# The attention's output product in three fp16 products instead of one fp32 product, with its scales, parts and squares placed among other work

## The chip, the cores and the metric

One core of one Trainium2 chip runs the whole program. The time is the device time of one execution in microseconds (us); less is better. TensorE (PE) multiplies, VectorE (DVE), ScalarE (ACT) and GpSimd (POOL) do elementwise work, SyncE (SP) starts most transfers.

## What is computed

Two graph layers on `x` (1250 rows of 512 features) with 20000 edges. The change is in the first one. Cut to what matters:

```python
h = relu(layernorm(x))                                   # layer 0 works on h
agg = segment_sum(batchnorm(h)[src], dst) / max(deg, 1)
conv_out = relu(agg @ W_conv + b_conv)
q, k, v = heads(h_dense @ Wq), heads(h_dense @ Wk), heads(h_dense @ Wv)   # h_dense: 256 rows
kv = einsum(phi(k), v);  z = 1 / (phi(q) @ sum(phi(k)) + KEPS)
attn = (einsum(phi(q), kv) * z) @ Wo                      # 256x512 @ 512x512
x = x + batchnorm(conv_out + attn[batch, pos] + h)
# layer 1: x + relu(bn(relu(bn(((1+eps) h + sum of h[src]) @ W1 + b1)) @ W2 + b2)), h = relu(layernorm(x))
```

## The kernel before, in words

TensorE counts the edges into a 1250x1250 matrix `AT`: 25 windows of 50 columns (line 1816), ten small fp16 matmuls each. Between windows stand pieces of the attention and the convolution. The order is the hand-written table `SLOTS` (line 79): one string a window. `G0` to `G9` are the ten tiles of the convolution, `K`, `Q`, `V` the projections, `UK`, `UQ`, `MX`, `QT`, `KV`, `O` the pieces of each pair of heads, `A00` to `A33` the aggregation by feature block and columns, `TA0` and `TA1` the transposes of `attn`, `WO0` and `WO1` the product with Wo. Each engine walks the table in this order in its own program, every queue strictly in order, and they meet at semaphores: `full` and `free` of the eight PSUM banks, and `s_...` of single steps.

- ACT (line 801) does in a slot: the pieces' copies out of PSUM, then the copy of `AT`, then extra work by a slot number (`conv_weights_high`, `weight_squares`, `weight_high`), and last the exponentials of `UQ` and `MX`, which are called late. `QT0` on PE (slot 8) transposes what the exponentials of `UQ0` wrote (slot 6) and waits for both heads of it (`s_eq`, line 1752). `G0` stands behind it in slot 9 and waits for POOL's `hn` (line 576).
- DVE (line 1290) makes the one-hot rows of the windows, reductions, the low parts and the sums into `hT`. After the windows it does `weight_low(0, 1)` (line 1140), `aggregate_terms()` (1148 to 1152) and the pieces of the last slot `TA0 TA1 A21 WO0 WO1` and of `LAST`, `A31 F2 DX2 A02 A12 A22 A23 A32 A33`.
- Most products are already split: `split3` (PE) sums hi·hi, hi·lo and lo·hi of fp16 parts. The product with Wo is not: `wA` and `attnT` are fp32, and each fp32 matmul is two instructions in the trace.

```python
for j in range(2):
    f = 2 * int(name[2]) + j
    for k in range(FB):
        ins = mm(ps[:, j * MAXN:(j + 1) * MAXN], wA[:, k, f * P:(f + 1) * P], attnT[:, k, :],
                 k == 0, k == FB - 1)
```

`F1` is the small product that sums the squares of W1 over the partitions for its scale; its square is taken by `weight_squares` on ACT and its inverse root by POOL (586, 587).

Of the kernel before, what the change touches and what calls it, by code (L numbers as in the profile page):

```python
# [63 lines left out]
for _n, _k in PARAMS:  # L64
# [14 lines left out]
SLOTS = [s.split() for s in (  # L79
# [4 lines left out]
SQ_AT, SPLIT_AT, H_AT, EDGES_OF_AT = 4, 7, 7, 18  # L84

SPARE = {"start": 18, "hT0": 3, "hT1": 4}
# [22 lines left out]
def unit_cols(name):  # L109
# [12 lines left out]

PAIR_BANKS = {f"UK{g}": (2, 3) for g in range(4)} | {f"{u}{g}": (4, 5) for g in range(4) for u in ("UQ", "QT")}
LONE_BANKS = {name: bank for bank, names in enumerate((
# [3 lines left out]
    for name in names.split()}  # L128
# [52 lines left out]

SQ1_AT, HIGH1_AT = (20, 21), (23, 24)
RAW = [name for slot in SLOTS for name in slot if name[0] == "A"]
OUT_TILES = [(0, 4), (4, 8), (8, 10)]

# [33 lines left out]
def gnn_kernel(nc, x, src, dst, params, eps, w_conv, wq, wk, wv, wo, proj, w1, w2, out):  # L221
    with ExitStack() as ctx:
# [95 lines left out]
        wB = place("wB", [P, FB, D], F32, 162)  # L318
        vaug = place("vaug", [P, 2, HEADS, DH + 1], F32, 170)
        attn = place("attn", [P, 2, D], F32, 174.25)  # L320
        attnT = place("attnT", [P, FB, MAXN], F32, 178.25)
        HR = T
        hring = place("hring", [L, HR, D], F32, 182.25)
        x_in = [place(f"x_in{n}", [L, 2, D], F32, at) for n, at in enumerate((45, 49, 53, 57, 61))]
# [179 lines left out]
        def _(pool):  # L504
# [75 lines left out]
            pool.wait_ge(sem("s_bn0"), 2)  # L580
            for i in range(T):
                normed(i)
            for layer in range(2):
                pool.wait_ge(sem(f"s_mean_w{layer}"), 1)
                m, s = mean_w[layer], scale_w[layer]
                own.step(pool.tensor_scalar(m[:, 1:2], m[:, 0:1], 1e-30, None, ALU.add))  # L586
                pool.tensor_tensor(s[:, 0:1], m[:, 1:2], minus_half[:, 0:1], ALU.pow).then_inc(sem(f"s_scale_w{layer}"), 1)
# [54 lines left out]
        def _(act):  # L642
# [25 lines left out]
            def attention(name):  # L668
# [14 lines left out]
                elif name in ("Q0", "Q1", "K0", "K1"):  # L683
                    a, f = "QK".index(name[0]), 2 * int(name[1])
                    ps = read_group(act, name)[:].rearrange("p (f n) -> p f n", f=2)
                    copy(tqk[:, a, f:f + 2, :], ps, SCALE).then_inc(sem("s_tqk"), 1)
                    free_group(act.activation(sq[:, a, f:f + 2, :], ps, ACT.Square, scale=SCALE), name)
                elif name[:2] == "MX":
                    g = int(name[2])
                    act.wait_ge(sem("s_nbk"), g + 1)  # L690
                    if g == 0:
                        act.wait_ge(full[PLACE["hT9"][0]], PLACE["hT9"][1] + 1)
                    if g >= 2:
                        act.wait_ge(full[PLACE[f"KV{g - 2}"][0]], PLACE[f"KV{g - 2}"][1] + 1)
                    for j, h in enumerate(heads_of(name)):
                        ps = read_group(act, f"UK{g}.{j}")
                        act.activation(kf[:, h % 4, 0, :], ps[:, 0:M], ACT.Exp, bias=nbk[:, h, 0:1])
                        act.activation(kf[:, h % 4, 1, :], ps[:, M:], ACT.Exp, bias=nbk[:, h, 1:2])\
                           .then_inc(sem("s_ek"), 1)
                    for j, h in enumerate(heads_of(name)):  # L700
                        act.wait_ge(sem("s_ek"), h + 1)
                        act.sem_inc(free[PLACE[f"UK{g}.{j}"][0]], 1)
                        act.activation(kf[:, h % 4], kf[:, h % 4], ACT.Identity, bias=keps[:, 0:1], scale=1.0 / 16)\
                           .then_inc(sem("s_kf"), 1)
                elif name[:2] == "UQ":
                    g = int(name[2])
                    if g:
                        act.wait_ge(full[PLACE[f"QT{g - 1}.1"][0]], PLACE[f"QT{g - 1}.1"][1] + 1)
                    else:
                        act.wait_ge(full[PLACE["hT5"][0]], PLACE["hT5"][1] + 1)  # L710
                    for j, h in enumerate(heads_of(name)):
                        act.wait_ge(sem("s_nbq"), h + 1)
                        ps = read_group(act, f"UQ{g}.{j}")
                        act.activation(qf[:, h % 2, 0, :], ps[:, 0:M], ACT.Exp, bias=nbq[:, h, 0:1])
                        act.activation(qf[:, h % 2, 1, :], ps[:, M:], ACT.Exp, bias=nbq[:, h, 1:2])\
                           .then_inc(sem("s_eq"), 1)
                        act.wait_ge(sem("s_eq"), h + 1)
                        act.sem_inc(free[PLACE[f"UQ{g}.{j}"][0]], 1)
                elif name[:2] == "KV":
                    g = int(name[2])  # L720
                    ps = read_group(act, name)
                    free_group(copy(kv[:, 2 * g:2 * g + 2], ps[:, 0:4 * (DH + 1)]
                                    .rearrange("p (h m d) -> p h m d", h=2, m=2)), name)
                elif name[:2] == "QT":
                    g = int(name[2])
                    if g:
                        act.wait_ge(full[PLACE[f"O{g - 1}"][0]], PLACE[f"O{g - 1}"][1] + 1)
                    for j in range(2):
                        ps = read_group(act, f"{name}.{j}")
                        free_group(act.activation(qfT[:, j], ps[:].rearrange("p (m n) -> p m n", m=2), ACT.Identity,  # L730
                                                  bias=keps[:, 0:1], scale=1.0 / 16), f"{name}.{j}")
                elif name[:2] == "TA":
                    nt = int(name[2])
                    ps = read_group(act, name)
                    free_group(copy(attnT[:, :, nt * P:(nt + 1) * P],
                                    ps[:].rearrange("p (f n) -> p f n", f=FB)), name)

            def conv_weights():
                act.wait_ge(sem("d_wC"), 16)
# [2 lines left out]
            def conv_weights_high():  # L742
                act.wait_ge(sem("s_wscale"), 1)
                act.activation(wC_hi[:], wC[:], ACT.Identity, scale=wscale[:, 0:1]).then_inc(sem("s_wch"), 1)

            def weight_squares(layer, half):
                raw_w, junk = ((w1_s, sq1), (w2_s, sq2))[layer]
# [53 lines left out]
            for t in range(len(SLOTS)):  # L801
# [22 lines left out]
                    copy(at_of(AT, t), counts_of(t)).then_inc(sem("s_at"), 1)  # L824
                if "FR" in SLOTS[t]:
                    conv_weights_high()
                if t in SQ1_AT:
                    if t == SQ1_AT[0]:
                        act.wait_ge(full[PLACE["UQ3.1"][0]], PLACE["UQ3.1"][1] + 1)
                    weight_squares(0, SQ1_AT.index(t))  # L830
                if t in HIGH1_AT:
                    weight_high(0, HIGH1_AT.index(t))
                for name in SLOTS[t]:
                    if late(name):
                        attention(name)
# [148 lines left out]
        def _(dve):  # L984
# [82 lines left out]
            def attention(name):  # L1067
# [48 lines left out]
                elif name[0] == "D":  # L1116
# [3 lines left out]
                    dve.wait_ge(free[PLACE[name][0]], PLACE[name][1] + 1)  # L1120
                    own.step(dve.tensor_scalar(d, d, 1.0, wscale[:, 0:1], ALU.max, ALU.mult))
                    n_deg[0] = own.mark(dve.reciprocal(d, d))
                elif name[:2] == "WO":
                    g = 2 * int(name[2])
                    ps = read_group(dve, name)[:].rearrange("p (f n) -> p f n", f=2)
                    own.step(dve.tensor_copy(att255[:, g:g + 2], ps[:, :, MAXN - 1]))
                    for f in (g, g + 1):
                        own.mark(dve.scalar_tensor_tensor(hT[:, f, 0:MAXN], ps[:, f - g, :], att255[:, f:f + 1],
                                                          hT[:, f, 0:MAXN], ALU.subtract, ALU.add))
                    own.after(own.n)  # L1130
                    dve.sem_inc(free[PLACE[name][0]], 1)

            n_deg = [0]

            def weight_low(layer, half):
# [3 lines left out]
                ks = slice(k * half, k * half + k)  # L1139
                dve.scalar_tensor_tensor(lo[:, ks, :], raw_w[half][:], scale_w[layer][:, 0:1], hi[:, ks, :],  # L1140
                                         ALU.mult, ALU.subtract).then_inc(sem(f"s_w{layer + 1}l"), 1)

            def aggregate_terms():

# [145 lines left out]
            for t in range(NW):  # L1290
# [26 lines left out]
                    normed_parts(t - H_AT - 1)  # L1317
                for name in SLOTS[t]:
                    piece(name)
                    if name == "O3":  # L1320
                        weight_low(0, 0)
            low_counts(NW - 1)
            weight_low(0, 1)
            aggregate_terms()
            for name in SLOTS[NW] + LAST:
                piece(name)
# [188 lines left out]
        def _(pe):  # L1515
# [75 lines left out]
            def attention(name):  # L1591
                if name == "FR":
                    pe.wait_ge(sem("s_ssq"), 1)
                    close_group(mm(open_group(pe, name)[:, 0:1], ssq[:].broadcast_to([P, P]), ones32[:], True, True), name)
                    return
                if name in ("F1", "F2"):
                    layer = int(name[1]) - 1
                    pe.wait_ge(sem(f"s_ssq_w{layer}"), 2)
# [177 lines left out]
                    for f in range(FB):  # L1776
                        ins = pe.transpose(ps[:, f * P:(f + 1) * P], attn[:, nt, f * P:(f + 1) * P], ident[:])
                elif name[:2] == "WO":
                    pe.wait_ge(sem("d_wA"), 32)
                    released("TA0")  # L1780
                    released("TA1")
                    ps = open_group(pe, name)
                    for j in range(2):
                        f = 2 * int(name[2]) + j
                        for k in range(FB):
                            ins = mm(ps[:, j * MAXN:(j + 1) * MAXN], wA[:, k, f * P:(f + 1) * P], attnT[:, k, :],
                                     k == 0, k == FB - 1)
                close_group(ins, name)

            def accumulate(groups, start):  # L1790
# [243 lines left out]
```

## Time and profile before

| | |
|---|---|
| median of 3 runs | 333.11 us (333.05 to 333.86) |
| the profiled execution | 333.72 us |
| its span, first to last instruction | 331.9 us |
| PE busy | 323.9 us, 98% |
| DVE / ACT / POOL busy | 214.7 / 166.5 / 116.9 us |
| granted TensorE clock, mean | 0.997 |

The profile is one execution of its own. Its time is its span and 1.8 us around it. Busy time is a sum over instructions. Matmuls are pipelined: a row's duration is longer than its distance to the next row's start, and this distance is what a matmul costs in a dense row. PEld are the weight loads, which run beside.

### The profile page before, as it was taken

What the parts mean: (1) busy time and instruction counts of PE and PEld (TensorE: products, weight loads), DVE (VectorE), ACT (ScalarE), POOL (GpSimd) and SP (SyncE); (2) the same over time, 40 slices, a digit from 0 to 9 for tenths busy, and PEclk for the clock granted to TensorE, in tenths of its full rate; (3) what the DMA queues carried; (4) which work ended last, traced back from release to release, by engine and by line L of the source; (5) the groups of instructions that cost most, each with busy time, mean ns of one, the idle gap of its engine ahead of it and who ended that gap; (6) DMA issues with size and microseconds to landing.
All of it is one profiled execution on the core that took longest, in us unless ns stands there. A gap on an engine that the chain in (4) does not pass through costs nothing.

```text
span 331.9 us, 5782 instructions
## 1 busy us (share of the span) xinstructions
PE 323.9 (98%) x2112; PEld 210.9 (64%) x2112; DVE 214.7 (65%) x462; ACT 166.5 (50%) x268; POOL 116.9 (35%) x200
## 2 busy tenths in 40 slices
PE   8999999999999999999999999999999999999994
PEld 3788666777676666777866755555555555566562
DVE  4799998879989589966789746125663453332235
ACT  3459776462471693726588646124434553413042
POOL 7034189552100010011356867322666452101100
PEclk9999999999999999999999999999999999999998
DMA  7994316000000000747000000000000000020314
GB/s 202 279 248 157 129 26 231 0 2 1 2 3 2 2 3 1 253 126 188 2 0 3 0 2 2 2 2 0 1 2 1 0 3 0 0 64 15 79 29 125
DMA packets 14008, 18.15 MB, mean 55 GB/s; under 512 B 1558, under 2 KB 7888, under 8 KB 13972
## 3 DMA queue, kind: packets, MB, share of 16 engines
q1 hardware_dynamic: 13636, 17.41, 18.6%
q8 instruction: 23, 0.38, 0.5%
q10 hardware_dynamic: 336, 0.26, 0.3%
q14 instruction: 13, 0.11, 0.1%
HBM read 15.10 MB, written 2.56 MB: 53 GB/s over the span
## 4 chain that ended last, share of the span: by engine, by line
PE 86%; DVE 5%; POOL 3%; ACT 2%; issue 1%; DMA 1%; SPq 0%; DVEq 0%; ACTq 0%; POOLq 0%
PE bank L1517 81%; PE bank L1554 2%; POOL hn L576 1%; DVE st L1175 1%; DMA x_in<-x 1%; PE bank L1973 1%; PE bank L1902 1%; PE bank L1757 1%; POOL ln_s L536 1%; DVE x L1465 0%; ACT hh L873 0%; DVE kmax L1075 0%; SPq L435 0%; DVE st_f L1165 0%; POOL bn_tmp L545 0%
## 5 line engine op out<-in xcount | busy, mean ns | idle before, releaser
L1517 PE MATMUL bank<-AT,hh 125*128 125x400 f16 (+4 forms) x260 | 81.4, 326 | 0.6 <-DVE hl L1362 0.6
L1517 PE MATMUL bank<-AT,hl 125*128 125x400 f16 (+4 forms) x260 | 81.1, 325 | 0.0
L1517 PEld LDWEIGHTS bank<-AT,hh 125*128 125x128 f16 x260 | 25.3, 97 | 18.0 <-DVE hl L1362 1.1
L1517 PEld LDWEIGHTS bank<-AT,hl 125*128 125x128 f16 x260 | 25.3, 97 | 16.6
L1517 PE MATMUL bank<-a_hi,w_hi 128*128 128x400 f16 (+3 forms) x96 | 32.6, 339 | 0.0
L1517 PE MATMUL bank<-agg_hi,w_hi 128*128 128x400 f16 (+1 forms) x96 | 32.6, 339 | 0.0
L1517 PE MATMUL bank<-a_hi,w_lo 128*128 128x400 f16 (+3 forms) x96 | 32.5, 339 | 0.0
L1517 PE MATMUL bank<-agg_hi,w_lo 128*128 128x400 f16 (+1 forms) x96 | 32.5, 338 | 0.0
L1517 PE MATMUL bank<-a_lo,w_hi 128*128 128x400 f16 (+3 forms) x96 | 32.5, 338 | 0.0
L1517 PE MATMUL bank<-agg_lo,w_hi 128*128 128x400 f16 (+1 forms) x96 | 32.5, 338 | 0.0
L626 POOL TENSOR_TENSOR a_lo<-zr,a_hi 128x1250 f16<-128x1250 f32 x7 | 22.0, 3141 | 16.7 <-DVE a_hi L1431 16.7
L928 ACT ACTIVATE zr<-bank,par,undo_w 128x400 f32<-128x400 f32 (+1 forms) x24 | 16.0, 690 | 23.5 <-POOL a_lo L626 17.1
L545 POOL TENSOR_TENSOR bn_tmp<-var_eps,minus_half 128x1 f32<-128x1 f32 (+1 forms) x15 | 8.7, 581 | 48.7 <-DVE var_eps L1189 48.7
L576 POOL TENSOR_SCALAR hn<-hT,bn_s,bn_t 128x125 f32<-128x125 f32 x36 | 20.9, 596 | 14.0 <-DVE hn_lo L1183 14.0
L1165 DVE BATCH_NORM_STATS2 st_f<-zr 128x6 f32<-128x400 f32 (+1 forms) x24 | 13.5, 588 | 18.1 <-ACT zr L928 18.1
L952 ACT ACTIVATE ur<-bank,par,undo_w 128x400 f32<-128x400 f32 (+3 forms) x12 | 8.2, 698 | 32.4 <-PE bank L1517 22.2
L536 POOL TENSOR_TENSOR ln_s<-ln_tmp,minus_half 125x1 f32<-125x1 f32 x20 | 14.3, 714 | 24.8 <-DVE ln_tmp L989 24.8
L586 POOL TENSOR_SCALAR mean_w<-mean_w 128x1 f32<-128x1 f32 x2 | 0.9, 446 | 62.3 <-ACT mean_w L652 62.3
L1060 DVE TENSOR_TENSOR S<-iota_code,lane 128x1280 f16<-128x1280 f16 x25 | 20.4, 816 | 0.6 <-DVE code L1032 0.2
L1165 DVE BATCH_NORM_STATS2 st_f<-ur 128x6 f32<-128x400 f32 (+1 forms) x9 | 5.2, 593 | 21.2 <-ACT ur L952 21.2
L1417 DVE SCALAR_TENSOR_TENSOR aggf<-bank,agg_terms,hT 128x400 f32<-128x400 f32 (+1 forms) x12 | 7.8, 652 | 15.2 <-PE bank L1517 10.5
L1060 DVE TENSOR_TENSOR ring<-iota_code,code 128x1000 f16<-128x1000 f16 x25 | 16.9, 675 | 0.0
(223 smaller groups left out, 709.0 us busy)
## 6 DMA issues: line engine op xcount, KB each, us to landing
w_s<-w SPq DMA_DIRECT2D x4, 1024.0 KB, 5.0
x<-x SPq DMA_DIRECT2D x2, 1120.0 KB
x_in<-x SPq DMA_DIRECT2D x3, 448.0 KB
out<-x SPq DMA_DIRECT2D x6, 224.0 KB
wB<-wk SPq DMA_DIRECT2D x2, 512.0 KB, 7.1
wA<-wq SPq DMA_DIRECT2D x1, 1024.0 KB, 11.4
wC<-w_conv SPq DMA_DIRECT2D x1, 1024.0 KB, 11.7
wB<-wv SPq DMA_DIRECT2D x1, 1024.0 KB, 9.3
```

The source lines that it names most:

```text
L536: own.step(pool.tensor_tensor(s, ln_tmp[:, 0, i:i + n], minus_half[0:L, 0:n], ALU.pow))
L545: own.step(pool.tensor_tensor(bn_tmp[:, 1, k:k + n], var_eps[:, k:k + n], minus_half[:, 0:n], ALU.pow))
L576: ins = pool.tensor_scalar(hn[:, i % 2, f, :], hT[:, f, i * L:(i + 1) * L], s[:, f:f + 1], b[:, f:f + 1], ALU.mult, ALU.add)
L626: pool.tensor_tensor(a_lo[:, b, :], zr[:, b % 2, :], a_hi[:, b, :], ALU.subtract)\
L928: ins = act.activation(zr[:, b % 2, c0:c0 + w], ps[:, 0:w], ACT.Identity, bias=pcol("b1", b), scale=undo_w[0][:, 0:1])
L952: ins = act.activation(ur[:, f % 2, c0:c0 + w], ps[:, 0:w], ACT.Identity, bias=pcol("b2", f), scale=undo_w[1][:, 0:1])
L1060: ins = dve.tensor_tensor(o[:, t % 2].rearrange("p j (q d) -> p j q d", d=2), pairs(iota_code[:, 0:n]).unsqueeze(1).broadcast_to(shape), v ...
L1165: return dve.bn_stats(st_f[:, f, ci, :], ap)
L1175: own.mark(dve.bn_stats(st_1[:, f, group, :], hT[:, f, a * L:b * L]))
L1417: ins = dve.scalar_tensor_tensor(aggf[:, k % 4, 0:w], ps[:, 0:w], agg_terms[:, 1:2], hT[:, f, c0:c0 + w], ALU.mult, ALU.add).then_inc(sem( ...
L1517: return pe.matmul(o, l, r, start=start, stop=stop, skip_group_check=True)
L1554: ins = pe.transpose(ps[:, f * L:(f + 1) * L], rows[:, i % slots, f * P:(f + 1) * P], ident[0:L, 0:L])
```

## The change

The product with Wo becomes a `split3`: both operands are scaled by an inverse root mean square and split into a high and a low fp16 part, 48 fp16 matmuls instead of 16 fp32 ones, and the result is scaled back on DVE. For the scales ACT squares Wo in slot 6 and V in slot 16, PE sums the squares in a new piece `FO` in slot 19, POOL takes the roots, ACT writes `wo_hi` in slot 19, DVE `wo_lo` in two halves in slots 20 and 21. The second half of w1 is split after `attnT` instead of ahead of it, on ACT and on DVE.

```diff
-    "MX2 G8", "QT2 G9", "KV2 UK3 D0", ...
+    "MX2 G8", "QT2 G9", "KV2 UK3 FO D0", ...
+SQO_AT, SQV_AT, HIGHO_AT = 6, 16, 19
+LOWO_AT = {"A00": 0, "MX3": 1}
-SQ1_AT, HIGH1_AT = (20, 21), (23, 24)
+SQ1_AT, HIGH1_AT = (20, 21), (23, 25)
...
# POOL
+            pool.wait_ge(sem("s_mean_o"), 1)
+            own.step(pool.tensor_tensor(mean_o[:, 0:1], mean_o[:, 0:1], mean_o[:, 2:3], ALU.add))
+            own.step(pool.tensor_scalar(mean_o[:, 0:2], mean_o[:, 0:2], 1e-30, None, ALU.add))
+            pool.tensor_tensor(scale_o[:], mean_o[:, 0:2], minus_half[:, 0:2], ALU.pow).then_inc(sem("s_scale_o"), 1)
...
# ACT, piece TA
-                    free_group(copy(attnT[:, :, nt * P:(nt + 1) * P],
-                                    ps[:].rearrange("p (f n) -> p f n", f=FB)), name)
+                    act.activation(attnT_hi[:, :, nt * P:(nt + 1) * P], ps[:].rearrange("p (f n) -> p f n", f=FB),
+                                   ACT.Identity, scale=scale_o[:, 0:1]).then_inc(sem("s_attnh"), 1)
+                    if nt:
+                        weight_high(0, 1)
...
+            def output_squares():
+                act.wait_ge(sem("d_wA"), 32)
+                act.activation(sqo[:], wA[:], ACT.Square, accum_out=ssq_o[:, 1:2]).then_inc(sem("s_ssq_o"), 1)
+            def value_squares():
+                for nt in range(2):
+                    act.wait_ge(sem("s_ssq_o"), 1 + nt)
+                    act.activation(sqv[:], vaug[:, nt].rearrange("p h d -> p (h d)"), ACT.Square, accum_out=ssq_o[:, 2 * nt:2 * nt + 1])\
+                       .then_inc(sem("s_ssq_o"), 1)
+            def output_weights():
+                act.wait_ge(sem("s_scale_o"), 1)
+                act.activation(wo_hi[:], wA[:], ACT.Identity, scale=scale_o[:, 1:2]).then_inc(sem("s_wo"), 1)
...
# ACT, in the loop over the slots
                 if "FR" in SLOTS[t]:
                     conv_weights_high()
+                if t == SQO_AT:
+                    output_squares()
+                if t == SQV_AT:
+                    value_squares()
+                if t == HIGHO_AT:
+                    output_weights()
...
# DVE
+                elif name[:2] == "TA":
+                    nt = int(name[2])
+                    dve.wait_ge(sem("s_attnh"), nt + 1)
...
+                    free_group(dve.scalar_tensor_tensor(attnT_lo[:, :, columns], ps, scale_o[:, 0:1], attnT_hi[:, :, columns],
+                                                        ALU.mult, ALU.subtract), name)
+                    if nt:
+                        weight_low(0, 1)
...
-                        own.mark(dve.scalar_tensor_tensor(hT[:, f, 0:MAXN], ps[:, f - g, :], att255[:, f:f + 1],
-                                                          hT[:, f, 0:MAXN], ALU.subtract, ALU.add))
+                        own.mark(dve.tensor_scalar(att_out[:, f, :], ps[:, f - g, :], att255[:, f:f + 1], undo_o[:, 1:2],
+                                                   ALU.subtract, ALU.mult))
                     own.after(own.n)
                     dve.sem_inc(free[PLACE[name][0]], 1)
+                    own.mark(dve.tensor_tensor(hT[:, g:g + 2, 0:MAXN], att_out[:, g:g + 2, :], hT[:, g:g + 2, 0:MAXN], ALU.add))
...
             low_counts(NW - 1)
-            weight_low(0, 1)
             aggregate_terms()
...
# PE
+                if name == "FO":
+                    pe.wait_ge(sem("s_ssq_o"), 3)
+                    close_group(mm(open_group(pe, name)[:, 0:3], ones32[:].broadcast_to([P, P]), ssq_o[:], True, True), name)
...
-                    pe.wait_ge(sem("d_wA"), 32)
+                    pe.wait_ge(sem("s_wol"), 2)
...
-                        for k in range(FB):
-                            ins = mm(ps[:, j * MAXN:(j + 1) * MAXN], wA[:, k, f * P:(f + 1) * P], attnT[:, k, :],
-                                     k == 0, k == FB - 1)
+                        fs = slice(f * P, (f + 1) * P)
+                        ins = split3(ps[:, j * MAXN:(j + 1) * MAXN], MAXN, (lambda k: wo_hi[:, k, fs], lambda k: wo_lo[:, k, fs]),
+                                     (lambda k: attnT_hi[:, k, :], lambda k: attnT_lo[:, k, :]), range(FB))
```

In ACT's queue in slots 6 and 7, before: `qf` are the exponentials of `UQ0`, `vaug` the copy of V1, `AT` that of the counts, `kf` the exponentials of `MX0`.

```order
L652 ACTIVATE vaug<-bank 128x8x64
L652 ACTIVATE AT<-bank 125x10x50
L744 ACTIVATE wC_hi<-wC,wscale 128x2048
L714 ACTIVATE qf<-bank,nbq 128x256
L715 ACTIVATE qf<-bank,nbq 128x256
```

And now, at the same place:

```order
L669 ACTIVATE vaug<-bank 128x8x64
L669 ACTIVATE AT<-bank 125x10x50
L768 ACTIVATE wC_hi<-wC,wscale 128x2048
L773 ACTIVATE sqo,ssq_o<-wA 128x2048
L731 ACTIVATE qf<-bank,nbq 128x256
L732 ACTIVATE qf<-bank,nbq 128x256
```

The square of Wo stands ahead of the exponentials that `QT0` waits for.

In DVE's queue after the last window, before: `w_lo` is `weight_low(0, 1)`, and the rows on `tmpr`, `hT`, `st_f` are the piece `A21`.

```order
L1140 SCALAR_TENSOR_TENSOR w_lo<-w_s,scale_w,w_hi 128x2048
L1148 TENSOR_SCALAR agg_terms<-eps_col 128x1
L1149 SCALAR_TENSOR_TENSOR agg_terms<-agg_terms 128x1
L1150 TENSOR_SCALAR agg_terms<-agg_terms 128x1
L1151 RECIPROCAL agg_terms<-agg_terms 128x1
L1152 TENSOR_TENSOR agg_terms<-agg_terms 128x1
L1248 TENSOR_TENSOR tmpr<-raw,rdb 128x400
L1255 SCALAR_TENSOR_TENSOR hT<-tmpr,neg_bc,hT 128x400
L1165 BN_STATS st_f<-hT 128x6
L1126 COPY att<-bank 128x2
L1128 SCALAR_TENSOR_TENSOR hT<-bank,att,hT 128x256 x2
```

And now, from the second of the small terms on:

```order
L1216 SCALAR_TENSOR_TENSOR agg_terms<-agg_terms 128x1
L1217 TENSOR_SCALAR agg_terms<-agg_terms 128x1
L1218 RECIPROCAL agg_terms<-agg_terms 128x1
L1219 TENSOR_TENSOR agg_terms<-agg_terms 128x1
L1175 SCALAR_TENSOR_TENSOR attnT_lo<-bank,scale_o,attnT_hi 128x4x128 x2
L1197 SCALAR_TENSOR_TENSOR w_lo<-w_s,scale_w,w_hi 128x2048
L1315 TENSOR_TENSOR tmpr<-raw,rdb 128x400
L1322 SCALAR_TENSOR_TENSOR hT<-tmpr,neg_bc,hT 128x400
L1232 BN_STATS st_f<-hT 128x6
L1182 COPY att<-bank 128x2
L1184 TENSOR_SCALAR att_out<-bank,att,undo_o 128x256 x2
L1188 TENSOR_TENSOR hT<-att_out,hT 128x2x256
```

The small terms stay ahead, the two low parts of `attnT` come next, and w1's low part moves behind them.

## Rows read from the trace of the kernel before

**Rows 1.** The page: busy time of the engines, and the last chain by engine.
```profile
PE 323.9 (98%) x2112; PEld 210.9 (64%) x2112; DVE 214.7 (65%) x462; ACT 166.5 (50%) x268; POOL 116.9 (35%) x200
...
PE 86%; DVE 5%; POOL 3%; ACT 2%; issue 1%; DMA 1%; SPq 0%; DVEq 0%; ACTq 0%; POOLq 0%
```

**Rows 2.** Timeline of PE, then PEld, 47 to 50 us: start, duration, instruction.
```profile
47.89 1.09 PE L1757 MATMUL bank<-ident,qf 128*128 128x128 f32 x8
48.82 0.61 PE L1517 MATMUL bank<-ring,S 128*128 128x100 f16 x10
...
49.58 0.29 PEld L1517 LDWEIGHTS bank<-wC,hn 128*125 128x125 f32 x2 [0.31 <-POOL hn L576]
```

**Rows 3.** The chain that ended last, in order of time: start, duration, what.
```profile
44.63 4.92 POOL hn L576 x4
```

**Rows 4.** Timeline of ACT, 36 to 48 us.
```profile
36.17 1.90 ACT L740 ACTIVATE sqr<-wC 128x2048 f32<-128x2048 f32 x1
...
38.06 1.05 ACT L652 ACTIVATE AT<-bank 125x500 f16<-125x500 f32 x2
...
47.37 0.47 ACT L715 ACTIVATE qf<-bank,nbq 128x256 f32<-128x256 f32 x1
```

**Rows 5.** Timeline of PE, 133 to 159 us.
```profile
133.93 0.33 PE L1517 MATMUL bank<-AT,hh 125*128 125x400 f16 x1
...
137.32 7.07 PE L1517 MATMUL bank<-attnT,wA 128*128 128x256 f32 x32
144.22 0.33 PE L1517 MATMUL bank<-AT,hh 125*128 125x400 f16 x1
...
154.75 0.25 PE L1517 MATMUL bank<-AT,hh 125*128 125x200 f16 x1
...
158.18 0.27 PE L1517 MATMUL bank<-AT,hh 125*128 125x250 f16 x1
```

**Rows 6.** Timeline of PE, 120 to 121 us: the piece `F1`.
```profile
120.36 0.50 PE L1517 MATMUL bank<-ones,ssq_w 128*128 128x1 f32 x4
120.72 0.61 PE L1517 MATMUL bank<-ring,S 128*128 128x100 f16 x10
```

**Rows 7.** Timeline of DVE, 134 to 152 us.
```profile
134.97 0.58 DVE L1165 BATCH_NORM_STATS2 st_f<-hT 128x6 f32<-128x400 f32 x1
135.75 2.35 DVE L1140 SCALAR_TENSOR_TENSOR w_lo<-w_s,scale_w,w_hi 128x2048 f16<-128x2048 f32 x1 [0.20 <-ACT w_hi L764]
138.02 0.15 DVE L1148 TENSOR_SCALAR agg_terms<-eps_col 128x1 f32<-128x1 f32 x1
...
139.17 0.58 DVE L1248 TENSOR_TENSOR tmpr<-raw,rdb 128x400 f32<-128x400 f32 x1 [0.23 <-DVE agg_terms L1152]
...
141.17 0.88 DVE L1128 SCALAR_TENSOR_TENSOR hT<-bank,att,hT 128x256 f32<-128x256 f32 x2
...
145.65 2.22 DVE L1165 BATCH_NORM_STATS2 st_f<-hT 128x6 f32<-128x450 f32 x4 [0.15 <-DVE hT L1128]
...
151.63 0.57 DVE L1253 TENSOR_TENSOR tmpr<-bank,rdb 128x400 f32<-128x400 f32 x1 [1.88 <-PE bank L1517]
```

**Rows 8.** Timeline of ACT, 135 to 137 us.
```profile
135.62 1.07 ACT L652 ACTIVATE attnT<-bank 128x512 f32<-128x512 f32 x2
```

**Rows 9.** Timelines of ACT, then DVE, with the idle time ahead in brackets.
```profile
91.54 0.60 ACT L652 ACTIVATE hh<-bank 125x512 f16<-125x512 f32 x1 [2.48 <-PE bank L1517]
...
106.50 0.55 ACT L652 ACTIVATE raw<-bank 128x450 f32<-128x450 f32 x1 [6.18 <-PE bank L1517]
...
110.95 0.63 DVE L1248 TENSOR_TENSOR tmpr<-raw,rdb 128x450 f32<-128x450 f32 x1 [1.97 <-ACT raw L652]
...
115.71 0.43 DVE L1121 TENSOR_SCALAR rdb<-rdb,wscale 128x400 f32<-128x400 f32 x1 [1.44 <-ACT rdb L652]
```

**Rows 10.** Windows by engine: us, busy PE, PEld, DVE, ACT, POOL, then granted clock, DMA.
```profile
327.00:328.00 1.00, 0.78 (x7) 0.59 (x6) 1.00 (x3) 0.14 (x1) 0.00 (x0) 1.00 0.00 1
...
330.00:331.00 1.00, 0.00 (x0) 0.00 (x0) 0.00 (x0) 0.00 (x0) 0.00 (x0) 0.61 0.80 220
```

More of the change, by code:

```diff
@@ L320, in gnn_kernel @@
         attn = place("attn", [P, 2, D], F32, 174.25)
-        attnT = place("attnT", [P, FB, MAXN], F32, 178.25)
+        attnT_hi = place("attnT_hi", [P, FB, MAXN], F16, 178.25)
+        attnT_lo = place("attnT_lo", [P, FB, MAXN], F16, 180.25)
+        att_out = place("att_out", [P, FB, MAXN], F32, 174.25)
+        wo_hi = place("wo_hi", [P, FB, D], F16, 88)
+        wo_lo = place("wo_lo", [P, FB, D], F16, 104)
+        sqo = place("sqo", [P, FB, D], F32, 57)
+        sqv = place("sqv", [P, HEADS * (DH + 1)], F32, 146)
+        ssq_o = place("ssq_o", [P, 3], F32, 85.28125)
+        mean_o = place("mean_o", [P, 3], F32, 85.3125)
+        scale_o = place("scale_o", [P, 2], F32, 85.375)
+        undo_o = place("undo_o", [P, 2], F32, 85.40625)
         HR = T
@@ L734, in attention @@
                     ps = read_group(act, name)
-                    free_group(copy(attnT[:, :, nt * P:(nt + 1) * P],
-                                    ps[:].rearrange("p (f n) -> p f n", f=FB)), name)
+                    act.activation(attnT_hi[:, :, nt * P:(nt + 1) * P], ps[:].rearrange("p (f n) -> p f n", f=FB),
+                                   ACT.Identity, scale=scale_o[:, 0:1]).then_inc(sem("s_attnh"), 1)
+                    if nt:
+                        weight_high(0, 1)
+                elif name == "FO":
+                    ps = read_group(act, name)
+                    copy(mean_o[:], ps[:, 0:3], 1.0 / (D * D)).then_inc(sem("s_mean_o"), 1)
+                    act.wait_ge(sem("s_mean_o"), 1)
+                    act.sem_inc(free[PLACE[name][0]], 1)
             def conv_weights():
@@ L830, in _ @@
                     weight_squares(0, SQ1_AT.index(t))
-                if t in HIGH1_AT:
-                    weight_high(0, HIGH1_AT.index(t))
+                if t == HIGH1_AT[0]:
+                    weight_high(0, 0)
                 for name in SLOTS[t]:
@@ L1122, in attention @@
                     n_deg[0] = own.mark(dve.reciprocal(d, d))
+                elif name[:2] == "TA":
+                    nt = int(name[2])
+                    dve.wait_ge(sem("s_attnh"), nt + 1)
+                    ps = banks[PLACE[name][0]][:].rearrange("p (f n) -> p f n", f=FB)
+                    columns = slice(nt * P, (nt + 1) * P)
+                    free_group(dve.scalar_tensor_tensor(attnT_lo[:, :, columns], ps, scale_o[:, 0:1], attnT_hi[:, :, columns],
+                                                        ALU.mult, ALU.subtract), name)
+                    if nt:
+                        weight_low(0, 1)
                 elif name[:2] == "WO":
@@ L1141, in weight_low, with output_weights_low @@
                                          ALU.mult, ALU.subtract).then_inc(sem(f"s_w{layer + 1}l"), 1)
+            def output_weights_low(half):
+                dve.wait_ge(sem("s_wo"), 1)
+                ks = slice(2 * half, 2 * half + 2)
+                ins = dve.scalar_tensor_tensor(wo_lo[:, ks, :], wA[:, ks, :], scale_o[:, 1:2], wo_hi[:, ks, :],
+                                               ALU.mult, ALU.subtract)
+                ins.then_inc(sem("s_wol"), 1)
+                if half:
+                    own.step(dve.tensor_tensor(undo_o[:, 0:1], scale_o[:, 0:1], scale_o[:, 1:2], ALU.mult))
+                    own.mark(dve.reciprocal(undo_o[:, 1:2], undo_o[:, 0:1]))
             def aggregate_terms():
@@ L1319, in _ @@
                     piece(name)
+                    if name in LOWO_AT:
+                        output_weights_low(LOWO_AT[name])
                     if name == "O3":
@@ L1595, in attention @@
                     return
+                if name == "FO":
+                    pe.wait_ge(sem("s_ssq_o"), 3)
+                    close_group(mm(open_group(pe, name)[:, 0:3], ones32[:].broadcast_to([P, P]), ssq_o[:], True, True), name)
+                    return
                 if name in ("F1", "F2"):
```

4 rows, old and new, of tables (LONE_BANKS, SLOTS) are left out of this document.

## The prediction, made before the changed kernel was run

> **What bounds the kernel now.** I read the page first. PE is busy 98% of the span, and the chain that ended last runs on PE for 86% [rows 1]. So a PE instruction removed from a dense stretch is worth its distance to the next, and work on another engine costs nothing until PE waits for it. The change touches three stretches, so next come their timelines. The first is 47 to 50 us. `QT0` starts at 47.89 [rows 2], and the last exponential it needs ends on ACT at 47.37 + 0.47 = 47.84 [rows 4]: ACT already releases it. The window's count follows at 48.82, then `G0`, whose weight load sat idle 0.31 us until POOL's `hn` was there [rows 2], at 44.63 + 4.92 = 49.55 [rows 3]. That is all the slack PE has there; behind `G0` the chain stays on PE. The second is 137 to 145 us: 32 instructions of the product with Wo, dense, between `A21` and `A31` [rows 5]. The third is DVE beside it [rows 7].
>
> The measurement of this kernel can tell a change from none at about 0.3%, 1.0 us.
>
> **The change, part by part.**
>
> *The product with Wo.* Before, from 137.32 to 144.22: 6.90 us [rows 5]. After, 48 fp16 matmuls of 256 columns. No row has this width, so I interpolate between dense ones: 40 matmuls of 200 columns from 154.75 to 158.18, 85.8 ns each; 20 of 400 columns from 133.93 to 137.32, 169.5 ns each [rows 5]. That is 0.419 ns a column, and 85.8 + 56 x 0.419 = 109 ns for 256. 48 x 109 ns = 5.24 us, so -1.66. Bounds: at the 200-column pace 4.12 us (-2.78), at the 400-column pace 8.14 us (+1.24); the width lies next to 200 and cost rises with columns, so I keep the line.
> A rule weighed here: the dense rows show 169.5 ns at 400 columns, on the line of columns over 2.4 GHz. The Trainium skill (TensorE: Matmul & The Clock Gate, section Back-to-back issue gap) also gives a sustained roofline in real kernels of about 81 ns at 128 columns and 131 ns at 512. Between these 256 columns would take about 98 ns by an estimate, 4.7 us in all, and the sum would be 0.5 us lower. By that rule 400 columns would take about 117 ns; the trace disagrees with 169.5.
>
> *`FO`.* `F1` is two such products in four instructions and takes 120.72 - 120.36 = 0.36 us [rows 6]. `FO` is one: +0.18, on PE in a dense stretch. Its inputs and bank are long there (below).
>
> *The square of Wo on ACT in slot 6.* The square of the convolution's weights has the same 128x2048 shape; the next instruction starts 38.06 - 36.17 = 1.89 us after it, accumulator read included [rows 4]. It stands ahead of the exponentials of `UQ0`, so the last of them ends at 49.73 and not 47.84. Wo's transfer starts behind `Q1` in slot 3, three windows earlier, so the square finds it there. ACT is in order; queued behind are the exponentials, V1's copy, the copy of `AT` and `MX0`'s exponentials. `QT0` then starts 1.89 us later, the count behind it too, and `G0`, which had 0.31 us to spare, 1.58 us later: +1.58. V1's copy, which frees `G0`'s bank, is next behind the exponentials and ends at about 50.5, ahead of `G0` at 51.2. Nothing in the PE rows after that gives it back. Below: 0, if some cover hides it all; above: 1.89, if `hn` came later too. I take 1.58, since both ends of it are read directly.
>
> *The squares of V in slot 16.* Two of 520 elements, by the same row about a quarter of 1.9 us plus a read each, some 1.3 us. ACT sat idle 2.48 us there for PE [rows 9]. Cost 0; without this cover `hh` of `G8` and the next count would be late.
>
> *Scales, `wo_hi`, `wo_lo`.* POOL is free between slots 16 and 22. Its three small operations, then `wo_hi` (about 2.0 us, slot 19), fall into ACT's 6.18 us of idle time ahead of 106.50 [rows 9]. Each half of `wo_lo` is half of the 2.35 us of `w_lo` [rows 7], 1.2 us; DVE sat idle 1.97 us where the first goes and 1.44 us where the second goes [rows 9], which with the two small `undo` terms may be over by 0.1 us, five microseconds ahead of anything that PE needs from DVE. Cost 0.
>
> *The low parts of `attnT`.* This is the new wait. PE reaches `WO0` at 137.32 in the old frame. ACT's two `attnT` copies, 1.07 us [rows 8], move ahead of the 2 us of w1's high half and start 1.9 us earlier, at 133.7, and are done by 134.8. DVE ends its statistics at 134.97 + 0.58 = 135.55; w1's low half (2.35) moves away, but `aggregate_terms` stays ahead, 139.17 - 138.02 = 1.15 us [rows 7], to 136.70. A low part: two PSUM operations of 256 columns take 0.88 us, 0.44 each, and `w_lo` of 2048 takes 2.35 [rows 7], so 1.07 ns a column and 0.71 us for 512, overlapping by 0.08. Two end at 136.70 + 0.63 + 0.71 = 138.04. PE waits 0.7 us: +0.72. Bounds: 0 if DVE's terms overlapped, 1.4 if a low part took 1.05 us; I take the middle, as its parts have rows.
>
> *DVE behind it.* w1's low half (to 140.3), `A21` (1.9, to 142.2), two groups of `WO` sums that grow from about 1.2 to 1.85 us (a separate 512-column add each; to 145.9), four statistics of 2.22 us [rows 7] to 148.1, `A31` to 150.0. `A02` on PE is done about 150.5 in that frame (138.04 + 5.24, then 3.4 each for `A31` and `A02` and 0.4 for `F2`). Before, DVE idled 1.88 us for `A02` [rows 7]; that is nearly used up, but not exceeded, and ends there. The banks of `F2` and `A33` come free in time. The transfer of `x` starts when `WO1` is done and w1's low parts are, so no later than PE moves. Cost 0; up to 0.3 if DVE were behind, since it has idle time again before the next piece.
>
> *Sum.* -1.66 + 0.18 + 1.58 + 0.72 = +0.82. The profiled execution, 333.72, becomes 334.5. It stands 0.6 above the median of the three runs, and the terms are differences, so the median goes from 333.11 to 333.9, 0.25% slower: within what can't be told from no change.
>
> **The rivals.**
>
> 1. *The square of Wo costs nothing.* For it: ACT is busy only half of the span [rows 1]. Against: an average says nothing of the one place; there the exponentials follow without a gap and PE follows them within 0.05 us [rows 2, 4]. Should it hold, -1.66 + 0.18 + 0.72 = -0.76: 332.4, still within 0.3%. If DVE's low parts came without a wait as well, 331.6, faster.
>
> 2. *DVE is late at the end of the windows.* The same squares and sums leave DVE behind, or a PSUM read with an fp16 operand is slower than the line; PE waits 1.4 us at `WO0` and 0.3 us at `A02`. It decides once DVE's second low part ends after 138.3. For: from 134.97 to 141.17 DVE's largest gap is the 0.23 us of a wait on itself [rows 7]. Against: every operation has a row. 333.9 + 1.0 = 334.9: slower.
>
> 3. *The clock falls in the new gap.* At the end of this trace PE stops at 327.8 and the granted clock is 1.00 until 330 and 0.61 in the next us [rows 10], so it fell after some 2.5 us of idle PE. The new gap before `QT0` is 1.9 us. If the clock fell to the 1.2 GHz level, `QT0`, the count and part of `G0` (5 us in all) would take up to twice as long: between 1.4 (the first two) and 5.0 more; I take 2, 335.9: slower. The Trainium skill (TensorE: Matmul & The Clock Gate, section Part 1: The HAM clock gate) says that TensorE's clock is gated to half after idleness, and its section Part 4: PE-mode transpose that transposes don't count as busy, which speaks against this change, as `QT0` is made of them; no row here shows the second.
>
> 4. *The change does less on PE than it says:* the narrow matmuls go at the pace of their weight loads or at the 200-column pace. At 85.8 ns the product takes 4.12 us and the time is 332.8. Against: matmuls of 200, 250 and 400 columns all lie on one line. The skill's roofline would put it at 333.4.
>
> **How the numbers follow.** Forecast as summed, 0.62; rival 1, 0.10; rival 2, 0.17; rival 3, 0.06; rival 4, 0.05. The forecast's own uncertainty is some 0.4 us: the wait at `WO0` and a few tenths of stalls. The range reaches from 332.6, which takes in rival 4 and the upper part of rival 1, to 335.0, which takes in rival 2. Slower begins at 334.1: most of rivals 2 and 3 and a quarter of the forecast's own spread, 0.39. Faster ends at 332.1: a part of rival 1, 0.08. Within: 0.53.
>
> **What would show it.** In the changed profile: a gap of about 1.9 us on PE ahead of the first `qf` transposes, with ACT's square of `wA` ending at about 47.9, and `G0` at 51.2; one more product in slot 19 worth 0.2 us; the 48 matmuls at 109 ns; a gap of 0.7 us before them, released by DVE's second low part, not by ACT; DVE at `A31` without idle time. I am wrong if PE doesn't wait at `QT0`, if `hn` comes later than 49.6, if the clock drops at 48 to 50 us, or if DVE, not PE, releases the pieces from `A02` on.

## The result, and the profile after

The changed kernel takes 334.44 us (median of 22 runs, 333.73 to 335.51), the kernel before 333.54 (22 runs, 333.01 to 334.33). The ratio is 1.0029 with a 95% interval of 1.0021 to 1.0036: 0.97 us slower by the ratio (0.70 to 1.20; the medians differ by 0.90). That is just under the 1.0 us that the prediction took for the least that can be told from no change; with 22 runs each the interval excludes 1, so the small loss is real. The forecast was +0.82, within the range and within its likeliest case.

On the page of the changed kernel, part 1 and the granted clock by slices, PE does 1.1 us less work than before in a span that is 0.7 us longer [rows 1]:

```profile
PE 322.8 (97%) x2130; PEld 209.8 (63%) x2130; DVE 220.2 (66%) x470; ACT 172.2 (52%) x276; POOL 117.5 (35%) x203
...
PEclk9999999999999999999999999999999999999998
```

So the loss is waiting, and the timelines say where. PE from 47 to 51 us (start, duration, instruction, idle time ahead and its releaser):

```profile
47.07 0.61 PE L1585 MATMUL bank<-ring,S 128*128 128x100 f16 x10
49.48 1.09 PE L1829 MATMUL bank<-ident,qf 128*128 128x128 f32 x8 [1.79 <-ACT qf L732]
50.41 0.61 PE L1585 MATMUL bank<-ring,S 128*128 128x100 f16 x10
50.86 3.66 PE L1585 MATMUL bank<-wC,hn 128*125 128x512 f32 x8
```

Against [rows 2]: `QT0` waits 1.79 us, released by ACT's exponential, and `G0` no longer waits for POOL. ACT beside it:

```profile
42.82 0.60 ACT L669 ACTIVATE vaug<-bank 128x512 f32<-128x512 f32 x1 [3.96 <-PE bank L1585]
...
45.68 1.91 ACT L773 ACTIVATE sqo<-wA 128x2048 f32<-128x2048 f32 x1
47.48 0.20 ACT L773 ACTIVATION_READ_ACCUMULATOR sqo<-wA 128x1 f32 x1
47.57 0.47 ACT L731 ACTIVATE qf<-bank,nbq 128x256 f32<-128x256 f32 x1
...
48.95 0.47 ACT L732 ACTIVATE qf<-bank,nbq 128x256 f32<-128x256 f32 x1
```

From the square's start to the exponential's it is 47.57 - 45.68 = 1.89 us. The idle stretch that could have held it, 3.96 us, lies in the first row, ahead of V0's copy.

PE in slot 19 and at the product with Wo:

```profile
99.89 0.38 PE L1585 MATMUL bank<-ssq_o,ones 128*128 128x3 f32 x2
100.13 0.54 PE L1585 MATMUL bank<-edges_of,ones 128*128 128x450 f16 x2
```

```profile
138.58 0.33 PE L1585 MATMUL bank<-AT,hl 125*128 125x400 f16 x1
139.62 0.27 PE L1585 MATMUL bank<-attnT_hi,wo_hi 128*128 128x256 f16 x1 [0.71 <-DVE attnT_lo L1175]
...
144.75 0.27 PE L1585 MATMUL bank<-attnT_hi,wo_lo 128*128 128x256 f16 x1
144.86 0.33 PE L1585 MATMUL bank<-AT,hh 125*128 125x400 f16 x1
```

`FO` costs 0.24 us. The last matmul of `A21` would have been followed at 138.58 + 0.17 = 138.75; the product starts at 139.62, 0.87 us later (the 0.71 in the bracket is less, since a matmul's end is modelled). The 48 matmuls take 144.86 - 139.62 = 5.24 us, against 6.90 before [rows 5]. DVE beside it:

```profile
136.40 0.58 DVE L1232 BATCH_NORM_STATS2 st_f<-hT 128x6 f32<-128x400 f32 x1
136.89 0.14 DVE L1215 TENSOR_SCALAR agg_terms<-eps_col 128x1 f32<-128x1 f32 x1
...
137.95 1.41 DVE L1175 SCALAR_TENSOR_TENSOR attnT_lo<-bank,scale_o,attnT_hi 128x512 f16<-128x512 f32 x2 [0.15 <-DVE agg_terms L1219]
...
149.45 0.56 DVE L1320 TENSOR_TENSOR tmpr<-bank,rdb 128x400 f32<-128x400 f32 x1
...
152.26 0.57 DVE L1320 TENSOR_TENSOR tmpr<-bank,rdb 128x400 f32<-128x400 f32 x1 [0.98 <-PE bank L1585]
```

The second low part ends at 139.36 and PE follows. `A31` (149.45) comes without idle time, `A02` with 0.98 us of it instead of 1.88 [rows 7]: DVE still waits for PE there.

**One zero for all traces.** Executions differ by some tenths of a us in their first 23 us and keep that offset: V0's copy on ACT starts at 43.13 in the trace before and at 42.82 in the one after. I read every later start from that copy. `A31` stands for the end of the product with Wo. The column on layer 1 is the start of the chain's long run of PE there (199.24 before, `91.91 PE bank x522`; in e1 the profile shows this run in two parts, and I take the start of the first, 198.18); the last column is its difference to the kernel before.

| from V0's copy, us | QT0 | G0 | WO0 | A31 | layer 1 | to before |
|---|---|---|---|---|---|---|
| before | 4.76 | 6.46 | 94.19 | 101.09 | 156.11 | |
| changed | 6.66 | 8.04 | 96.80 | 102.04 | 157.06 | +0.95 |
| e1, square early | 4.75 | 6.55 | 95.35 | 100.58 | 155.60 | -0.51 |
| e2, low parts first | 6.65 | 8.03 | 95.91 | 101.16 | 156.17 | +0.06 |
| e3, both | 4.77 | 6.47 | 94.44 | 99.69 | 154.72 | -1.39 |
| e4, square alone | 6.65 | 8.03 | 95.68 | 102.59 | 157.62 | +1.51 |
| e5, square twice | 8.68 | 10.47 | 100.49 | 105.73 | 160.75 | +4.64 |
| e6, FO five times | 6.65 | 8.04 | 97.70 | 102.94 | 158.59 | +2.48 |
| e7, w1 first | 6.66 | 8.04 | 99.38 | 106.28 | 161.30 | +5.19 |
| e8, e1 again | 4.75 | 6.45 | 95.23 | 100.47 | 155.48 | -0.63 |
| e9, e3 again | 4.76 | 6.46 | 94.41 | 99.65 | 154.66 | -1.45 |

The +0.95 of the second row fits the measured +0.97: within a tenth of a us, all of it has arisen by the start of layer 1.

### The profile page after: what moved, and what is told of

The parts are those of the page before. It is cut to its first block, busy times and chain, and to the rows that moved or that the text cites. A ratio compares the mean times of both kernels' runs of the same rounds, so it can differ in the third digit from the quotient of the medians.

```text
span 332.6 us, 5839 instructions
## 1 busy us (share of the span) xinstructions
PE 322.8 (97%) x2130; PEld 209.8 (63%) x2130; DVE 220.2 (66%) x470; ACT 172.2 (52%) x276; POOL 117.5 (35%) x203
## 4 chain that ended last, share of the span: by engine, by line
PE 70%; DVE 10%; ACT 8%; issue 4%; DMA 3%; SPq 2%; POOL 1%; DVEq 0%; ACTq 0%; POOLq 0%
PE bank L1585 66%; DMA x_in<-x 3%; ACT sq L792 1%; DVE st L1242 1%; PE bank L1622 1%; PE bank L2045 1%; SPq L447 1%; PE bank L1974 1%; ACT hring L680 1%; PE bank L1829 1%; DVE ring L1107 1%; DVE rdb L1169 1%; POOL ln_s L548 1%; ACT hT L669 1%; DVE hT L1322 1%
## 5 line engine op out<-in xcount | busy, mean ns | idle before, releaser
L588 POOL TENSOR_SCALAR hn<-hT,bn_s,bn_t 128x125 f32<-128x125 f32 x36 | 20.2, 575 | 15.8 <-DVE hn_lo L1250 14.8
```

Source lines behind the costliest of these rows:

```text
L588: ins = pool.tensor_scalar(hn[:, i % 2, f, :], hT[:, f, i * L:(i + 1) * L], s[:, f:f + 1], b[:, f:f + 1], ALU.mult, ALU.add)
```

## The experiments

Each ratio is against the kernel before, measured beside the run. What a run gains or loses against the changed kernel is the difference of two such ratios.

**e1: the square in the idle stretch.** The changed kernel with

```diff
                         act.wait_ge(sem("s_fr"), 1)
                         act.sem_inc(free[PLACE[name][0]], 1)
+                        output_squares()
...
-                if t == SQO_AT:
-                    output_squares()
```

> The changed kernel with one edit: ACT squares Wo right behind the copy of FR, in the stretch in which it idles 3.96 us for V0, and not behind conv_weights_high. My theory (the square holds QT0, and with it G0): QT0 starts 0.05 us after the exponentials as before, the gap on PE ahead of it goes, G0 starts when hn is there, and the time falls by 1.3 to 1.6 us against the changed kernel, to 0.9977 of the kernel before (332.8 us by its median of 333.54). If POOL or the clock made the stall, not the square, G0 stays where the changed kernel has it and the time stays at 1.003. The gap ahead of WO0, 0.87 us, stays in both.

Measured: 332.91 us, ratio 0.9993 (0.9976 to 1.0009); once more, as e8, 333.00 us, ratio 0.9992 (0.9983 to 1.0001).

> The kernel of e1_square_early once more, as its interval left 1 inside. My theory, by the differences read in its trace (product -1.66, low-part wait +0.88, FO +0.24): 0.5 us below the kernel before, ratio 0.9985; together with the first measurement below 1. If the square cost something beyond its stall, 0.9995 or more.

ACT in e1:

```profile
39.05 1.91 ACT L773 ACTIVATE sqo<-wA 128x2048 f32<-128x2048 f32 x1 [0.44 <-ACT wcol L669]
...
42.58 0.60 ACT L669 ACTIVATE vaug<-bank 128x512 f32<-128x512 f32 x1 [1.52 <-PE bank L1584]
```

ACT squares Wo and still idles 1.52 us for V0. `QT0` and `G0` stand where they stood before the change, so the square made the stall, not POOL or the clock. The time fell by 1.2 us against the changed kernel (1.0029 - 0.9993 = 0.0036), by 1.46 in the table and by 1.58 in e8's row; 1.3 to 1.6 was expected, and the intervals hold it. The expected ratio of 0.9977 was too low by itself: 1.3 to 1.6 us below 1.0029 is 0.9981 to 0.9990. The remaining gain over the kernel before, 0.5 to 0.6 us in the traces, isn't shown by the times: both intervals reach 1, also that of e8, which was run to bring it below.

**e2: the low parts ahead of the small terms.** The changed kernel with

```diff
-            aggregate_terms()
             for name in SLOTS[NW] + LAST:
...
                     if nt:
                         weight_low(0, 1)
+                        aggregate_terms()
```

> The changed kernel with one edit: DVE makes the two low parts of attnT ahead of aggregate_terms (five small operations, 1.06 us), not behind. My theory (PE's wait at WO0 is for DVE's second low part): it ends 1.06 us earlier, ahead of A21's end on PE, the gap of 0.87 us becomes 0 to 0.1, and the time falls by 0.7 to 0.9 us, to 1.0005 of the kernel before (333.7 us). If A02 and what follows are bound by DVE, whose queue stays as long, the gap ahead of WO0 goes and a gap behind it comes, and the time stays at 1.003.

Measured: 333.52 us, ratio 1.0003 (0.9989 to 1.0016). PE and DVE in e2:

```profile
138.06 0.33 PE L1585 MATMUL bank<-AT,hl 125*128 125x400 f16 x1
138.22 0.28 PE L1585 MATMUL bank<-attnT_hi,wo_hi 128*128 128x256 f16 x1
```

```profile
136.36 1.39 DVE L1175 SCALAR_TENSOR_TENSOR attnT_lo<-bank,scale_o,attnT_hi 128x512 f16<-128x512 f32 x2
137.81 2.35 DVE L1198 SCALAR_TENSOR_TENSOR w_lo<-w_s,scale_w,w_hi 128x2048 f16<-128x2048 f32 x1
140.08 0.15 DVE L1216 TENSOR_SCALAR agg_terms<-eps_col 128x1 f32<-128x1 f32 x1
```

The wait at `WO0` is gone, and 0.87 us arrives in the time (1.0029 - 1.0003), 0.89 in the table. No gap comes behind it. So five operations of 0.15 us, whose result is first read 35 us later (by ACT at 172.38 in the changed kernel's trace, on the way into layer 1), cost the changed kernel 0.9 us.

**e3: both edits.**

> Both edits in one kernel. If the two stalls lie one behind the other on PE and nothing else takes their place, their gains add: 2.0 to 2.5 us below the changed kernel, 1.4 us below the kernel before, ratio 0.9955 to 0.996 (332.1 us), which is the product's 1.66 us less FO's 0.24. If DVE is the next bound behind WO1, the gain is at least 0.5 us smaller than the sum of the two, and PE shows a gap in A02 to A33.

Measured: 331.86 us, ratio 0.9951 (0.9932 to 0.9970); once more, as e9, 332.03 us, ratio 0.9960 (0.9947 to 0.9973).

> The kernel of e3_both once more, beside the first on the same chip. My theory: 1.4 us below the kernel before, ratio 0.9958, and 0.9 us below the square alone moved.

```profile
47.05 1.09 PE L1828 MATMUL bank<-ident,qf 128*128 128x128 f32 x8
48.75 3.70 PE L1584 MATMUL bank<-wC,hn 128*125 128x512 f32 x8 [0.16 <-POOL hn L588]
```

```profile
149.39 0.56 DVE L1320 TENSOR_TENSOR tmpr<-bank,rdb 128x400 f32<-128x400 f32 x1
...
152.76 0.58 DVE L1320 TENSOR_TENSOR tmpr<-bank,rdb 128x400 f32<-128x400 f32 x1 [1.07 <-PE bank L1584]
```

The gains add: 0.95 + 1.39 = 2.34 us below the changed kernel in the table, 1.46 + 0.89 from the two alone. e9 is 0.97 us below e8, measured beside it; 0.9 was expected. This version beats both kernels, by 1.3 to 1.6 us against the kernel before. That is the product's 1.66 less `FO`'s 0.24, with both stalls gone. In the DVE rows, `A02` (149.39) now comes with no idle time ahead: DVE is late by the work that the change gave it. At the next piece it waits 1.07 us for PE again, so the delay ends there, as the prediction had it.

**e4: the square alone.** The kernel before with two tiles for the square's output and, behind `conv_weights_high()`,

```diff
+                    act.wait_ge(sem("d_wA"), 32)
+                    act.activation(sqo[:], wA[:], ACT.Square, accum_out=ssq_o[:, 1:2])
```

> The kernel before with nothing but the square of Wo added to ACT in slot 6, at the place where the change has it; nothing reads it. My theory: QT0 moves by 1.89 us, G0 by 1.3 to 1.6, the rest of the timeline with it, and the time by 1.3 to 1.6 us, ratio 1.004 to 1.0048 (335.0 us). If ACT's half-idle queue could cover it, the ratio is 1.000; if the changed kernel's loss came from the end of the windows, also 1.000.

Measured: 334.63 us, ratio 1.0036 (1.0021 to 1.0051), +1.2 us. One ACT instruction with no reader makes PE's program late: `G0` by 1.57 us, layer 1 by 1.51. Both lie in the expected 1.3 to 1.6, and the interval of the time holds them.

**e5: the square twice.** The changed kernel with

```diff
+                act.activation(sqo[:], wA[:], ACT.Square, accum_out=ssq_o[:, 1:2]).then_inc(sem("s_sqo_twice"), 1)
+                act.wait_ge(sem("s_sqo_twice"), 1)
                 act.activation(sqo[:], wA[:], ACT.Square, accum_out=ssq_o[:, 1:2]).then_inc(sem("s_ssq_o"), 1)
```

> The changed kernel with Wo squared twice, one behind the other, in slot 6: the suspected cost doubled, and a gap of some 3.8 us on PE ahead of QT0, longer than the 2.5 us of idleness behind which the clock had fallen at the end of the kernel before. My theory (every us of ACT ahead of the exponentials is a us on PE, clock untouched): QT0 and G0 1.9 to 2.1 us later than in the changed kernel, and the time as well, ratio about 1.009 (336.3 us). If idleness alone of this length brings the clock to its lower level, the granted clock shows about 0.5 between 49 and 55 us, G0 lasts longer than 3.6 us, and the time is 1.5 to 4 us higher still (1.013 to 1.02).

Measured: 338.83 us, ratio 1.0167 (1.0135 to 1.0198). `QT0` is 2.02 us later than in the changed kernel, as expected of the square. The time is 4.6 us more than the changed kernel's. PE, then windows of PE (us, busy, count, granted clock, DMA share, GB/s):

```profile
51.20 1.16 PE L1831 MATMUL bank<-ident,qf 128*128 128x128 f32 x8 [3.82 <-ACT qf L732]
52.16 1.04 PE L1587 MATMUL bank<-ring,S 128*128 128x100 f16 x10
52.99 4.91 PE L1587 MATMUL bank<-wC,hn 128*125 128x512 f32 x8
```

```profile
50.00:51.00 1.00, 0.00 (x0) 1.00 1.03 426
51.00:52.00 1.00, 0.80 (x7) 1.00 0.18 70
52.00:53.00 1.00, 1.00 (x14) 0.54 0.00 0
53.00:54.00 1.00, 1.00 (x5) 0.50 0.00 0
54.00:55.00 1.00, 1.00 (x3) 0.50 0.00 0
55.00:56.00 1.00, 1.00 (x3) 0.75 0.00 0
56.00:57.00 1.00, 1.00 (x4) 1.00 0.00 0
```

After a gap of 3.82 us the clock falls to its 1.2 GHz level from about 52 to 55.5 us, and `G0` takes 57.83 - 52.99 = 4.84 us instead of 3.59. It falls when PE has been working again for almost a us, not in the gap. In this execution the clock makes 3.69 - 2.02 = 1.67 us of the table's difference to the changed kernel. The profiled run, 337.71, was the second shortest of the six. Its mean granted clock is 0.994 and that of the shortest 0.995; the four longer ones, 338.73 to 340.64, have 0.989 or 0.990, where those of the kernel before have 0.996 to 1.000. By these means the clock fell in all six and took more in the longer ones; where it fell there no trace shows. The Trainium skill (TensorE: Matmul & The Clock Gate, section Part 1: The HAM clock gate) says that idleness brings the half clock; the rows agree for this gap, and for the changed kernel's gap of 1.79 us they show 1.00 throughout.

**e6: `FO` five times.**

```diff
+                    for _ in range(4):
+                        mm(open_group(pe, name)[:, 0:3], ones32[:].broadcast_to([P, P]), ssq_o[:], True, True)
```

> The changed kernel with the small product FO issued five times. My theory (a product of three columns on PE costs its two passes with their weight loads, 0.18 us as read from F1, on the path): 0.7 to 0.8 us more than the changed kernel, ratio about 1.005. If it costs the 0.24 us seen once in the changed trace each time, 0.96 us more, ratio 1.0058. If it were hidden, 1.003.

Measured: 335.89 us, ratio 1.0067 (1.0043 to 1.0091), 1.3 us more than the changed kernel where 0.7 to 0.96 was expected; the interval, 0.5 to 2.1, reaches into that. PE in e6:

```profile
99.97 1.28 PE L1585 MATMUL bank<-ssq_o,ones 128*128 128x3 f32 x10
101.11 0.54 PE L1585 MATMUL bank<-edges_of,ones 128*128 128x450 f16 x2
```

Five take 1.14 us, 0.23 each, and `WO0` moves by 0.90 us, as four more products would have it. (Within that, `A21` ends 0.80 us later, and PE's wait at `WO0` is 0.97 us against 0.87.) Layer 1 has 0.62 us more, and the timeline shows where, behind four small products with `ident`:

```profile
201.50 0.36 PE L1585 MATMUL bank<-AT,hh 125*128 125x450 f16 x1 [0.62 <-issue]
```

At this one place PE waits for nothing that the profile shows. No other trace here has one of this length between 55 and 325 us. e1 has one of 0.20 us, 0.9 us into the same run of PE (199.11 where 198.91 was due), and e8, the same kernel, has none: so a small stall there can come and go between executions. Whether the added instructions bring e6's is open. Up to it e6 is 0.91 us behind the changed kernel.

**e7: w1 split ahead of `attnT`,** as before the change, on ACT and DVE:

```diff
-SQ1_AT, HIGH1_AT = (20, 21), (23, 25)
+SQ1_AT, HIGH1_AT = (20, 21), (23, 24)
...
-                    if nt:
-                        weight_low(0, 1)
...
+            weight_low(0, 1)
             aggregate_terms()
```

> The changed kernel with one part undone: the second half of w1 is split ahead of attnT, on ACT and on DVE, as in the kernel before. My theory (WO0 waits for DVE's second low part, wherever DVE's queue puts it): DVE ends it 2.35 us (w1's low half) and a wait of 0.2 us for ACT later, the gap ahead of WO0 grows from 0.87 to 3.2 to 3.5 us, and the time by 2.3 to 2.6 us, ratio about 1.010. If the reordering didn't matter, because PE waits for something else, the ratio stays at 1.003.

Measured: 338.26 us, ratio 1.0148 (1.0122 to 1.0174). PE, and windows of PE:

```profile
141.73 0.27 PE L1582 MATMUL bank<-attnT_hi,wo_hi 128*128 128x256 f16 x1 [3.28 <-DVE attnT_lo L1173]
```

```profile
141.00:142.00 1.00, 0.27 (x3) 1.00 0.63 244
142.00:143.00 1.00, 1.00 (x11) 1.00 0.11 43
143.00:144.00 1.00, 1.00 (x7) 0.50 0.00 0
```

The wait grew as expected, from 0.87 to 99.38 - 95.93 = 3.45 us. The time grew by 4.0, not 2.6. In the trace it is 4.24, of which 2.58 is the wait and 1.66 again the clock: it falls at 143 us, over a us after PE went back to work, and the same 48 matmuls take 6.90 us instead of 5.24. (That the fp32 product took 6.90 us too is chance.) Five of the six runs have a mean clock of 0.987 to 0.994; the shortest, 337.62, has 1.000, so the fall may not come every time. So the part of the change that put w1 behind `attnT` was needed, and it was worth more than its us on DVE.

## Why the prediction was right, step by step

| term | forecast | in the traces |
|---|---|---|
| product with Wo | -1.66 | -1.66 (e1 to e3 as well) |
| `FO` | +0.18 | +0.24; 0.23 each in e6 |
| square of Wo in slot 6 | +1.58 | +1.57 (e4 alone), undone in e1 |
| wait at `WO0` | +0.72 | +0.87, undone in e2 |
| the rest | 0 | -0.07, between `G0` and `WO0` |
| sum | +0.82 | +0.95; measured +0.97 |

- *The product.* The line through the 200- and 400-column rows gave 109 ns, and 48 took 5.24 us. The Trainium skill (TensorE: Matmul & The Clock Gate, section Back-to-back issue gap) gives about 81 ns at 128 columns and 131 ns at 512; the estimate of 98 ns between them would have been 0.5 us less. The trace of the changed kernel disagrees with it as the rows of before did.
- *The square.* Both halves of the argument held: the exponentials follow the square without a gap, and PE's slack was the 0.31 us at `G0` alone. That ACT was idle half of the time said nothing. Rival 1 asked for cover that only another place in the queue has, which e1 shows. e4 gets back 0.06 us behind `G0`, so the rest of -0.07 is already there with the square alone.
- *The wait at `WO0`* was the step that was mis-sized most, by 0.15 us. DVE itself was on time: its second low part ended 0.61 us after `A21` (139.36 against 138.75), where the forecast had 0.72. But PE's first matmul came 0.26 us after that end, and the sum had no term for this. A little luck hides in the 0.72: from the end of the statistics the small terms took 0.97 us instead of 1.15 and the two low parts 1.41 instead of 1.34, so DVE was 0.11 us earlier than forecast, which covers part of the 0.26.
- *`FO`* was taken as half of `F1`; it cost 0.05 to 0.06 more.
- *The terms of 0* held. ACT still idles 1.10 us behind V's squares (2.48 before) and 3.79 behind `wo_hi` (6.18 before), and DVE 0.99 us behind the first half of `wo_lo` (1.97 before). The second half takes up the whole 1.44 us, and what follows starts on time. PE shows no wait between `G0` and `WO0`.
- *DVE behind it* had more room than I gave it: 0.98 us of idle time ahead of `A02`.
- *Rival 2* had its place right, not its size: the wait is 0.87, not 1.4, and `A02` isn't late. *Rival 3* didn't happen at 1.79 us of idle time; e5 and e7 show that it can at 3.82 and 3.28. So at most 1.5 us of further idle time stood between the forecast and a loss that no term of the sum held. Where between 1.79 and 3.28 it begins, and whether the length of the gap alone decides, wasn't tried.
- The stalls' two edits together are worth 2.3 us, more than the product's own gain. So the answer "no difference to speak of" was a sum of large terms, not a change without effect.

## What to carry to other kernels

Before putting work into an engine's idle time, find the idle stretch in its timeline and put the work ahead of the instruction that ends it. One instruction later, the same work is in series with whatever follows, and here that cost all that the cheaper product gave. When a wait moves onto a queue, look at what small work that nobody needs yet still stands ahead of the awaited step. And count a long gap of PE for more than its length: in the two traces with gaps of 3.28 and 3.82 us, the clock took 1.7 us on top.

## What the runs showed of the hardware that I had not expected

- The clock can fall behind a gap. In e5 and in e7 it stayed at 1.00 through 3.82 and 3.28 us of idle PE and fell 0.9 and 1.3 us after PE was busy again, to half, until about 55.5 and 146.4 us. At the end of the kernel before it fell while PE was still idle, some 2.4 us after the last matmul [rows 10]. A trace that shows full clock in a gap does not say that the gap was free.
- From the end of a DVE low part (a PSUM bank and an fp16 tile in, fp16 out) to PE's first matmul it took 0.26 us in the changed kernel and in e7 (141.47 to 141.73), while from ACT's last exponential to `QT0` it took 0.06. What makes the difference wasn't tried.
